# Feed-forward layer of a float32 transformer block: two plain token tiles, then seven tile pairs by Strassen's seven products

## The chip, the cores and the metric

The kernel runs on one core of one Trainium2 chip. The metric is device time in microseconds (us) of one execution: 2028.8 us before the change, the median of 3 runs (2028.22 to 2028.88). Views of the profile come from one profiled execution of the same kernel. The engines are PE (TensorE, matmul; PEld is its weight load), ACT (ScalarE), DVE (VectorE), POOL (GpSimd) and SP (SyncE, whose queue issues nearly all DMAs here).

## The reference

The input x has 8 sequences of 1024 tokens with 512 channels, the context 8 x 64 keys with 384 channels; all is float32.

```python
x = x + attention(layernorm(x), ctx)        # 16 heads, output projection Wo, bias bo
xn = layernorm(x)
hidden = xn @ W1 + b1                       # 512 -> 2048
imag = w_imag * sin(phases + 0.1 * hidden)
gain = cos(phases) * w_real + sin(phases) * w_imag
act = relu(hidden + gain * imag * 0.1)
x = x + act @ W2 + b2                       # 2048 -> 512
```

## The kernel before, in words

Tokens are taken in 16 tiles (`TILES`) of 512 (`TOK`). First comes attention for all tiles, which leaves x plus attention in HBM (`x1_dram`); then the feed-forward layer, tile by tile. Every float32 product is made of three matmuls of fp32r operands (`product`, lines 1394 to 1396): each operand is split into a rounded part (`hi`, ScalarE) and the rest (`lo`, VectorE), and hi x hi, hi x lo and lo x hi are summed in PSUM.

The feed-forward layer has `FC` = 16 chunks of 128 hidden channels for each tile. All of W1 and W2, in hi and lo, stays in SBUF. The step j = 16 t + f does the following:

- TensorE: `h = W1[f] x xt` into bank f % 4: 4 blocks of input channels x 3 matmuls = 12 matmuls of 512 columns. Then `second(j - 3)`: act x W2[f] into banks 4 to 7, which hold the tile's 4 output blocks over all 16 chunks: 4 x 3 = 12 matmuls.
- ScalarE: `turns` (the phase in turns, from PSUM, line 1010), `hid` (from PSUM, line 1012), the sine (`sine`, line 995), the relu that is also the hi split (`finish`, line 1001).
- VectorE: the whole number of turns (line 1350), `hid += gain * sine` (`wave`, line 1320), the lo split (`finish`, line 1325).
- GpSimd: turns minus whole turns (line 820), between VectorE's line 1350 and ScalarE's sine.

Beside that, each tile has once: its rows from HBM, the biases (GpSimd, lines 637 and 645), statistics (VectorE, line 1049), normalising (ScalarE, line 865), a transposition that consists of 32 x 32 transposes (VectorE, lines 1379 and 1384) and a way through HBM in 128-byte pieces, the split into `xt_hi` and `xt_lo`, and four additions of the outputs (`residual`, line 1313).

The order on each engine is written out by hand in Python loops, one per engine; all sync is by counting semaphores. An engine's instructions run in the order of its list, and a wait holds everything behind it. Queue SP does the same with DMAs: each `dma_start` waits for its semaphores, and those behind it wait too. What limits how far TensorE runs ahead is PSUM (4 banks for `h`) and the ring of 4 `act` buffers (`ACTS`).

## Time and profile before

| what | value |
|---|---|
| median of the runs | 2028.8 us |
| the profiled execution's span | 2027.3 us |
| what lies around the span (median minus span) | 1.5 us |
| PE busy | 2014.9 us (99%) |
| DVE busy | 1342.4 us (66%) |
| ACT busy | 1131.6 us (56%) |
| POOL busy | 1021.5 us (50%) |
| DMA moved | 168.51 MB, mean 83 GB/s |

The profile's page begins with busy time by engine, gives it then in 40 equal slices, then the DMA queues, the chain of waits that ended last, and the costliest groups of instructions (line, engine, operation, output <- inputs, count, busy and mean time, idle time before them and who ended it). A matmul's duration is longer than the distance from one to the next, since they are pipelined; so the distance of starts is what to read. The feed-forward layer begins at 630.3 us. Attention before it is not changed but for a few DMAs.

### The profile page before, as it was taken

Reading aid. Unit: us, or ns where it says so; the run is one execution under the profiler, and the core shown is the slowest. Engines: PE = TensorE matmul, PEld = TensorE weight load, DVE = VectorE, ACT = ScalarE, POOL = GpSimd, SP = SyncE. Lnnn points to the kernel's source line nnn. Section 1 sums busy time; section 2 is a strip of 40 time slices with the busy share of each in tenths; the row PEclk is TensorE's granted clock in tenths of the full one; section 3 lists DMA queues with packets and bytes.
Section 4 is the critical chain, followed back from the end, with each engine's and each line's share of the span. In section 5 each row is a group of like instructions: output and inputs, shape, how many; then the busy total and the mean of one; then the engine's idle time right before and its main releaser. Section 6 shows DMA issues by size and latency. Waiting matters only on the chain.

```text
span 2027.3 us, 26664 instructions
## 1 busy us (share of the span) xinstructions
PE 2014.9 (99%) x9498; PEld 1684.9 (83%) x9498; DVE 1342.4 (66%) x1983; ACT 1131.6 (56%) x1979; POOL 1021.5 (50%) x708
## 2 busy tenths in 40 slices
PE   9999999999999999999999999999999999999999
PEld 7788888888888888888888888888888888888887
DVE  8988888888876665655555555565655555555554
ACT  6767767667665655544554454545545454554453
POOL 6877777777774453435334343433435334343521
PEclk9999999999999999999999999999999999999999
DMA  7565675655524311121111212211130211112100
GB/s 240 150 164 136 169 175 138 173 137 164 143 66 144 107 42 42 45 81 27 57 42 42 54 40 73 42 42 42 42 83 21 64 43 42 46 48 73 42 22 21
DMA packets 232822, 168.51 MB, mean 83 GB/s; under 512 B 154353, under 2 KB 184049, under 8 KB 232689
## 3 DMA queue, kind: packets, MB, share of 16 engines
q1 hardware_dynamic: 231824, 166.76, 29.8%
q8 instruction: 75, 1.23, 0.3%
q14 instruction: 59, 0.48, 0.1%
q10 hardware_dynamic: 864, 0.04, 0.0%
HBM read 98.34 MB, written 68.16 MB: 82 GB/s over the span
## 4 chain that ended last, share of the span: by engine, by line
PE 91%; DVE 4%; ACT 2%; POOL 1%; issue 1%; DMA 1%; SPq 0%; ACTq 0%; DVEq 0%; POOLq 0%
PE psum L1394 29%; PE psum L1396 29%; PE psum L1395 29%; PE psum L1487 2%; DVE hid L1320 1%; POOL prob L679 0%; DVE act_lo L1325 0%; POOL prob L700 0%; ACT act_hi L1001 0%; ACT hid L1012 0%; DVE top L1177 0%; DVE prob L1168 0%; DMA x_sb<-in_x 0%; DVE xt_lo L1067 0%; DVE xt_lo L1277 0%
## 5 line engine op out<-in xcount | busy, mean ns | idle before, releaser
L820 POOL TENSOR_TENSOR frac<-turns,frac 128x512 f32<-128x512 f32 x256 | 333.3, 1302 | 826.9 <-DVE frac L1350 826.9
L1320 DVE SCALAR_TENSOR_TENSOR hid<-frac,gain,hid 128x512 f32<-128x512 f32 x256 | 321.7, 1257 | 144.2 <-ACT frac L995 143.1
L1394 PE MATMUL psum<-w_hi,act_hi 128*128 128x512 f32 x1024 | 398.3, 389 | 0.0
L1395 PE MATMUL psum<-w_lo,act_hi 128*128 128x512 f32 x1024 | 398.3, 389 | 0.0
L1396 PE MATMUL psum<-w_hi,act_lo 128*128 128x512 f32 x1024 | 398.3, 389 | 0.0
L1010 ACT ACTIVATE turns<-psum,u_shift 128x512 f32<-128x512 f32 x256 | 176.5, 689 | 328.4 <-PE psum L1396 271.2
L1001 ACT ACTIVATE act_hi<-hid 128x512 fp32r<-128x512 f32 x256 | 161.8, 632 | 353.9 <-DVE hid L1320 353.9
L1325 DVE SCALAR_TENSOR_TENSOR act_lo<-hid,act_hi 128x512 fp32r<-128x512 f32 x256 | 197.6, 772 | 178.1 <-ACT act_hi L1001 178.1
L1350 DVE TENSOR_SCALAR frac<-turns 128x512 f32<-128x512 f32 x256 | 111.4, 435 | 248.1 <-ACT turns L1010 248.1
L1395 PEld LDWEIGHTS psum<-w_lo,act_hi 128*128 128x128 f32 x1024 | 192.3, 188 | 40.0
L1394 PEld LDWEIGHTS psum<-w_hi,act_hi 128*128 128x128 f32 x1024 | 192.1, 188 | 39.9
L1396 PEld LDWEIGHTS psum<-w_hi,act_lo 128*128 128x128 f32 x1024 | 192.1, 188 | 39.8
L1394 PE MATMUL psum<-xt_hi,w1a_hi 128*128 128x512 f32 x512 | 199.5, 390 | 0.5 <-DVE xt_lo L1067 0.3
L1396 PE MATMUL psum<-xt_hi,w1a_lo 128*128 128x512 f32 x512 | 199.2, 389 | 0.0
L1395 PE MATMUL psum<-xt_lo,w1a_hi 128*128 128x512 f32 x512 | 199.2, 389 | 0.0
L1396 PE MATMUL psum<-xt_hi,w1b_lo 128*128 128x512 f32 x512 | 199.2, 389 | 0.0
L1394 PE MATMUL psum<-xt_hi,w1b_hi 128*128 128x512 f32 x512 | 199.2, 389 | 0.0
L1395 PE MATMUL psum<-xt_lo,w1b_hi 128*128 128x512 f32 x512 | 199.2, 389 | 0.0
L1012 ACT ACTIVATE hid<-psum,par 128x512 f32<-128x512 f32 x256 | 174.5, 682 | 0.0
L995 ACT ACTIVATE frac<-frac 128x512 f32<-128x512 f32 x256 | 161.4, 630 | 0.0
L700 POOL TENSOR_TENSOR prob<-prob,top 128x1024 f32<-128x1024 f32 x64 | 122.1, 1907 | 73.2 <-DVE top L1177 73.1
L679 POOL TENSOR_TENSOR prob<-prob,inv 128x1024 f32<-128x1024 f32 x64 | 123.6, 1931 | 42.1 <-DVE inv L1159 42.0
(149 smaller groups left out, 4013.1 us busy)
## 6 DMA issues: line engine op xcount, KB each, us to landing
res<-in_x SPq DMA_DIRECT2D x64, 256.0 KB, 3.8
x_dram<-res SPq DMA_DIRECT2D x64, 256.0 KB, 3.1
x_sb<-in_x SPq DMA_DIRECT2D x15, 1024.0 KB, 6.4
x_sb<-x_dram SPq DMA_DIRECT2D x15, 1024.0 KB, 5.5
xn<-turn_dram SPq DMA_DIRECT2D x30, 512.0 KB, 5.1
out<-x_sb SPq DMA_DIRECT2D x15, 1024.0 KB, 4.4
turn_dram<-kt SPq DMA_DIRECT2D x112, 128.0 KB, 2.4
x_sb<-turn_dram SPq DMA_DIRECT2D x28, 512.0 KB, 6.3
```

What stands on the lines that cost most here:

```text
L679: pool.tensor_tensor(rows, rows, inv[:, (i - 1) % 2, :].unsqueeze(2) .to_broadcast([P, NB * HG, KEYS]), ALU.mult).then_inc(prob_done, 1)
L700: pool.tensor_tensor(rows, rows, top[:, i % 2, :].unsqueeze(2).to_broadcast([P, NB * HG, KEYS]), ALU.subtract).then_inc(shift_done, 1)
L820: pool.tensor_tensor(frac[:, j % 2, :], turns[:, j % 2, :], frac[:, j % 2, :], ALU.subtract)\
L995: act.activation(frac[:, j % 2, :], frac[:, j % 2, :], ACT.Sin, scale=SIN_SCALE).then_inc(sin_done, 1)
L1001: act.activation(act_hi[:, j % ACTS, :], hid[:, j % 2, :], ACT.Relu).then_inc(act_hi_done, 1)
L1010: act.activation(turns[:, j % 2, :], hidden, ACT.Identity, bias=u_shift[:, f:f + 1], scale=0.1 / TWO_PI).then_inc(turns_done, 1)
L1012: act.activation(hid[:, j % 2, :], hidden, ACT.Identity, bias=par[:, 3, f:f + 1])\
L1320: dve.scalar_tensor_tensor(out=hid[:, j % 2, :], in0=frac[:, j % 2, :], scalar=gain[:, f:f + 1], in1=hid[:, j % 2, :], op0=ALU.mult, op1=A ...
L1325: dve.scalar_tensor_tensor(out=act_lo[:, j % ACTS, :], in0=hid[:, j % 2, :], scalar=0.0, in1=act_hi[:, j % ACTS, :].bitcast(F32), op0=ALU. ...
L1394: pe.matmul(o, a_hi, b_hi, start=first, stop=False)
L1395: pe.matmul(o, a_hi, b_lo, start=False, stop=False)
L1396: return pe.matmul(o, a_lo, b_hi, start=False, stop=last)
```

## The change

The two plain tiles (0 and 1) keep the 16 steps of 24 matmuls. For the others, tiles 2T and 2T+1 form a pair (T = 1 to 7). The first product of the layer, W1 x xt, is seen as a 2 x 2 block product: two chunks of hidden channels x two halves of the input channels, times two halves of input channels x two tiles. Strassen's scheme needs 7 block products (`P1` to `P7`) of 6 matmuls each, in place of 8. A pair has 8 groups p (`FP`), each for hidden chunks 2p and 2p+1, of both tiles. So one group gives four chains of elementwise work (kinds 0 to 3: chunk 2p and 2p+1 of the first tile, then 2p+1 and 2p of the second).

TensorE's order in a group is P1, P6, P4, P2, P5, P7, then `second` of two chunks of the first tile that the group before made, then P3. The second tile's hidden chunks stay in SBUF (`late_hid`), and after the eighth group a sweep of `second` for all its chunks follows (14 of 16; the last two come in the next pair's first group).

What goes with that:

- The sums of W1 blocks are formed once, by GpSimd during the two plain tiles (`add_parts`: 4 for each group), split into hi and lo, and written to HBM (`w1s`); the unsummed parts are copied there too. W2, in hi and lo, is written to HBM (`w2s`). In the pairs W1's operands come back through a ring of 8 slots of 256 KB, one load for each product, and W2's through a ring of 4 slots of 512 KB, one load for each `second`.
- The sums of token operands (T1 to T4) are formed by GpSimd once for each pair, from 128x1024 tiles.
- The products' sums are finished by VectorE: five operations from PSUM in each group (`sum_u`, `sum_v`, `hidden_21`, `hidden_22`, `hidden_12`), and ScalarE copies P1 out of PSUM (`keep_p1`).
- GpSimd no longer takes part in the chain of each chunk. Rounding to whole turns moves from VectorE to ScalarE (`whole`), the subtraction from GpSimd to VectorE (`fraction`).
- The outputs have a buffer of their own (`acc`), filled by a further load of x1's rows.
- Part of the code under `If_ne` (rows with a NaN in attention) is rewritten; it is not executed with these inputs.

```diff
+PRODUCTS = ("P1", "P6", "P4", "P2", "P5", "P7", "P3")
+OPERANDS = ("B11", "B21", "T1", "T2", "T4", "T3", "B22")
+BANK_OF = {"P1": 0, "P2": 0, "P6": 1, "P7": 1, "P5": 2, "P3": 2, "P4": 3}
+W1_SLOTS = 8
+W2_SLOTS = 4
...
+        def events(T):                                # order on TensorE and SP
+            order = []
+            for p in range(FP):
+                i = (T - 1) * FP + p
+                order += [("product", i, name) for name in PRODUCTS[:-1]]
+                if p:
+                    order += [("second", first_half(T, 2 * p - 2), None), ("second", first_half(T, 2 * p - 1), None)]
+                else:
+                    order += [("second", second_half(T - 1, c), None) for c in range(SWEPT, FC)]
+                order.append(("product", i, PRODUCTS[-1]))
+            order += [("second", first_half(T, FC - 2), None), ("second", first_half(T, FC - 1), None)]
+            return order + [("second", second_half(T, c), None) for c in range(SWEPT if T + 1 < FFN_PAIRS else FC)]
...
+            def load_w1(n):                           # SP
+                if n >= W1_SLOTS:
+                    sp.wait_ge(prod, n - W1_SLOTS + 1)
...
+            def load_w2(e):                           # SP
+                c = e % FC
+                sp.wait_ge(f_psum, e - W2_SLOTS + 1)
...
+            for T in range(1, FFN_PAIRS):             # ScalarE
+                more = T + 1 < FFN_PAIRS
+                for p in range(FP):
+                    i = (T - 1) * FP + p
+                    keep_p1(i)
+                    if p:
+                        turn(i - 1, 3)
+                        positive(first_half(T, 2 * p - 1))
+                        sine(chain_at(i - 1, 3))
+                    turn(i, 0)
+                    hidden(i)
+                    for at, s, half in ((3, 0, 0), (3, 0, 1), (5, 1, 0), (5, 1, 1)):
+                        if more and p == at:
+                            ffn_rows(2 * T + 2 + s, half)
+                    sine(chain_at(i, 0))
+                    turn(i, 1)
+                    turn(i, 2)
+                    positive(first_half(T, 2 * p))
+                    sine(chain_at(i, 1))
+                    sine(chain_at(i, 2))
...
+                for p in range(FP):                   # VectorE
+                    i = (T - 1) * FP + p
+                    if p:
+                        hidden_12(i - 1)
+                        wave(chain_at(i - 1, 2))
+                    sum_u(i)
+                    if p == 1:
+                        add_outputs(2 * T - 1)
+                    if p:
+                        positive_lo(first_half(T, 2 * p - 1))
+                        fraction(chain_at(i - 1, 3))
+                        wave(chain_at(i - 1, 3))
+                    if more and p in (3, 5):
+                        layer_shift(TILES + 2 * T + 2 + p // 5)
+                    fraction(chain_at(i, 0))
+                    sum_v(i)
+                    hidden_21(i)
+                    hidden_22(i)
+                    wave(chain_at(i, 0))
+                    if more and p in (1, 2):
+                        layer_stats(TILES + 2 * T + 2, half_blocks(p - 1))
+                    if more and p in (3, 4):
+                        turn_late_rows(2 * T + 2, p - 3)
+                        layer_stats(TILES + 2 * T + 3, half_blocks(p - 3))
+                    if more and p in (5, 6):
+                        turn_late_rows(2 * T + 3, p - 5)
+                    fraction(chain_at(i, 1))
+                    fraction(chain_at(i, 2))
+                    positive_lo(first_half(T, 2 * p))
+                    wave(chain_at(i, 1))
...
+            def strassen(i, name):                    # TensorE
+
+                p, n, j = i % FP, at_prod(i, name) - 1, OPERANDS.index(MOVING[name])
+                pe.wait_ge(w1_in[n % W1_SLOTS], 16 * (n // W1_SLOTS + 2))
...
+                elif name == "P5" and i:
+                    pe.wait_ge(c12_done, i)
+                elif name == "P2":
+                    pe.wait_ge(p1_done, i + 1)
+                elif name == "P7":
+                    pe.wait_ge(u_done, i + 1)
+                elif name == "P3":
+                    pe.wait_ge(c22_done, i + 1)
```

ScalarE's list in a plain step of the kernel before (PSUM tile `h` is `psum`; one step's four instructions, and the next step's first):

```order
L1010 ACTIVATE turns<-psum,u_shift 128x512 [waits act_lo_done,frac_done,h_psum]
L1012 ACTIVATE hid<-psum,par 128x512
L995 ACTIVATE frac<-frac 128x512 [waits frac_done]
L1001 ACTIVATE act_hi<-hid 128x512 [waits f_psum,wave_done]
L1010 ACTIVATE turns<-psum,u_shift 128x512 [waits act_lo_done,frac_done,h_psum]
```

ScalarE's list in a group of a pair of the changed kernel, from kind 0's turns on (line 1384 is `whole`, 1408 `turn`, 1416 `hidden`, 1421 the sine, 1436 the relu, 1391 `keep_p1` of the next group):

```order
L1408 ACTIVATE turns<-psum,u_shift 128x512 [waits prod,frac_done]
L1384 ACTIVATE frac<-turns,round_col 128x512 [waits wave_done,turns_done]
L1416 ACTIVATE hid<-psum,par 128x512 [waits act_lo_done]
L1421 ACTIVATE frac<-frac 128x512 [waits frac_done]
L1408 ACTIVATE turns<-hid,p_shift 128x512 [waits c21_done,frac_done]
L1384 ACTIVATE frac<-turns,round_col 128x512 [waits wave_done,turns_done]
L1408 ACTIVATE turns<-late_hid,p_shift 128x512 [waits c22_done,frac_done]
L1384 ACTIVATE frac<-turns,round_col 128x512 [waits wave_done,turns_done]
L1436 ACTIVATE act_hi<-hid 128x512 [waits wave_done,f_psum]
L1421 ACTIVATE frac<-frac 128x512 [waits frac_done] x2
L1391 ACTIVATE p_sb<-psum 128x512 [waits v_done,prod]
```

Three of the four turns in a group now come from SBUF tiles that VectorE has written (the waits c21_done, c22_done, c12_done), where all came from PSUM; a further instruction, `whole`, stands between turns and VectorE's part.

VectorE's list in a plain step of the kernel before:

```order
L1350 TENSOR_SCALAR frac<-turns 128x512 [waits wave_done,turns_done]
L1320 SCALAR_TENSOR_TENSOR hid<-frac,gain,hid 128x512 [waits hid_done,sin_done]
L1325 SCALAR_TENSOR_TENSOR act_lo<-hid,act_hi 128x512 [waits act_hi_done]
L1350 TENSOR_SCALAR frac<-turns 128x512 [waits wave_done,turns_done]
L1320 SCALAR_TENSOR_TENSOR hid<-frac,gain,hid 128x512 [waits hid_done,sin_done]
```

VectorE's list around a border of two groups in the changed kernel (1834 is `fraction`, 1848 `wave`, 1855 the lo split, 1797 `sum_u`, 1805 `sum_v`, 1814, 1822 and 1829 the three `hidden_` sums, 1529 the shift of a later tile's rows):

```order
L1834 SCALAR_TENSOR_TENSOR frac<-frac,turns 128x512 [waits whole_done] x2
L1855 SCALAR_TENSOR_TENSOR act_lo<-hid,act_hi 128x512 [waits act_hi_done]
L1848 SCALAR_TENSOR_TENSOR hid<-frac,gain,hid 128x512 [waits sin_done]
L1829 TENSOR_TENSOR late_hid<-psum,late_hid 128x512 [waits u_done,prod]
L1848 SCALAR_TENSOR_TENSOR late_hid<-frac,gain,late_hid 128x512 [waits sin_done]
L1797 SCALAR_TENSOR_TENSOR late_hid<-psum,par,p_sb 128x512 [waits act_lo_done,p1_done,prod]
L1855 SCALAR_TENSOR_TENSOR act_lo<-hid,act_hi 128x512 [waits act_hi_done]
L1834 SCALAR_TENSOR_TENSOR frac<-frac,turns 128x512 [waits whole_done]
L1848 SCALAR_TENSOR_TENSOR late_hid<-frac,gain,late_hid 128x512 [waits sin_done]
L1529 SCALAR_TENSOR_TENSOR shift_rows<-mv,rstd 128x4 [waits rstd_done]
L1834 SCALAR_TENSOR_TENSOR frac<-frac,turns 128x512 [waits whole_done]
L1805 SCALAR_TENSOR_TENSOR late_hid<-psum,par,p_sb 128x512 [waits act_lo_done,prod]
```

The five sums from PSUM stand between the operations of the chains, and each of them releases a product of TensorE or a turn of ScalarE.

The SP queue in a group and at its border in the changed kernel (719 is `load_w1`, 745 `load_w2`, 701 and 707 the way of a turned tile through HBM):

```order
L719 DMA w_ring<-w1s 128x512 [waits prod] x7
L707 DMA x_sb<-turn_dram 128x16x64 [waits a_moved0]
L707 DMA x_sb<-turn_dram 128x16x64 [waits a_moved1]
L745 DMA w_ring<-w2s 128x1024 [waits w2_stored0,f_psum]
L745 DMA w_ring<-w2s 128x1024 [waits w2_stored1,f_psum]
L701 DMA turn_dram<-temps 32x4x256 [waits a_back0,a_turned]
L701 DMA turn_dram<-temps 32x4x256 x3
L719 DMA w_ring<-w1s 128x512 [waits prod] x7
```

Before, SP had between two tiles only the turned rows (8 + 2 DMAs), one store and one load; now 7 loads of W1 and 2 of W2 stand in each group, in TensorE's order.

## Rows read from the trace of the kernel before

**Rows 1.** The page: busy time, the clock by slices, the chain by engine.
```profile
PE 2014.9 (99%) x9498; PEld 1684.9 (83%) x9498; DVE 1342.4 (66%) x1983; ACT 1131.6 (56%) x1979; POOL 1021.5 (50%) x708
...
PEclk9999999999999999999999999999999999999999
...
PE 91%; DVE 4%; ACT 2%; POOL 1%; issue 1%; DMA 1%; SPq 0%; ACTq 0%; DVEq 0%; POOLq 0%
```

**Rows 2.** Windows: busy (x count) PE, PEld, DVE, ACT, POOL; clock, DMA share, GB/s.
```profile
630.30:673.00 42.70, 42.67 (x188) 35.37 (x189) 31.45 (x54) 28.46 (x50) 12.65 (x9) 1.00 0.32 100
...
1300.00:1400.00 100.00, 100.00 (x443) 82.80 (x442) 56.68 (x76) 50.11 (x83) 43.04 (x31) 1.00 0.20 52
```

**Rows 3.** Timeline, PE: first and last matmul of the feed-forward layer.
```profile
630.33 0.47 PE L1394 MATMUL psum<-xt_hi,w1a_hi 128*128 128x512 f32 x1 [0.26 <-DVE xt_lo L1067]
...
2023.53 0.39 PE L1396 MATMUL psum<-w_hi,act_lo 128*128 128x512 f32 x1
```

**Rows 4.** Timeline: one step of a tile; start, duration, idle before and releaser.
```profile
1305.45 0.39 PE L1396 MATMUL psum<-xt_hi,w1b_lo 128*128 128x512 f32 x1
...
1305.87 0.69 ACT L1010 ACTIVATE turns<-psum,u_shift 128x512 f32<-128x512 f32 x1 [1.71 <-PE psum L1396]
...
1306.46 0.68 ACT L1012 ACTIVATE hid<-psum,par 128x512 f32<-128x512 f32 x1
...
1307.03 0.63 ACT L995 ACTIVATE frac<-frac 128x512 f32<-128x512 f32 x1
...
1307.10 1.29 POOL L820 TENSOR_TENSOR frac<-turns,frac 128x512 f32<-128x512 f32 x1 [0.74 <-DVE frac L1350]
...
1307.69 1.24 DVE L1320 SCALAR_TENSOR_TENSOR hid<-frac,gain,hid 128x512 f32<-128x512 f32 x1 [0.67 <-ACT frac L995]
...
1308.97 0.63 ACT L1001 ACTIVATE act_hi<-hid 128x512 fp32r<-128x512 f32 x1 [1.31 <-DVE hid L1320]
...
1309.64 0.69 DVE L1325 SCALAR_TENSOR_TENSOR act_lo<-hid,act_hi 128x512 fp32r<-128x512 f32 x1 [0.70 <-ACT act_hi L1001]
```

**Rows 5.** Timeline: the last `wave`, with GpSimd idle.
```profile
2017.45 0.75 DVE L1320 SCALAR_TENSOR_TENSOR hid<-frac,gain,hid 128x512 f32<-128x512 f32 x1
```

**Rows 6.** One line's instructions each: ns min/median/max, first and last start.
```profile
L1320 DVE SCALAR_TENSOR_TENSOR hid<-frac,gain,hid x256: 735/1246/1834, 637.9 to 2017.4; 128x512 f32<-128x512 f32 x128
...
L1313 DVE TENSOR_TENSOR x_sb<-psum,x_sb x64: 675/681/692, 725.8 to 2024.0; 128x512 f32<-128x512 f32 x64
...
L1184 DVE TENSOR_TENSOR pt_lo<-psum,pt_hi x128: 629/681/695, 46.3 to 614.0; 128x512 fp32r<-128x512 f32 x128
...
L637 POOL TENSOR_TENSOR x_sb<-x_sb,bo_row x64: 1287/1739/1755, 616.3 to 1881.6; 128x512 f32<-128x512 f32 x64
...
L1049 DVE BATCH_NORM_STATS2 stats<-x_sb x128: 634/677/695, 3.8 to 1887.5; 128x6 f32<-128x512 f32 x128
...
L1379 DVE STREAM_TRANSPOSE stage<-xn x14: 1236/1237/1239, 771.7 to 1903.2; 128x1024 f32<-128x1024 f32 x14
...
L865 ACT ACTIVATE xn<-x_sb,shift_rows,rstd x64: 799/802/814, 625.1 to 1903.2; 128x512 f32<-128x512 f32 x64
```

**Rows 7.** Windows during one store of 1 MB, one load of 1 MB, the 128-byte pieces.
```profile
1339.00:1341.00 2.00, 2.00 (x10) 1.69 (x9) 1.14 (x2) 0.68 (x2) 0.00 (x0) 1.00 0.98 368
...
1344.00:1347.00 3.00, 3.00 (x15) 2.49 (x14) 1.15 (x3) 2.10 (x4) 0.23 (x1) 1.00 0.86 322
...
1310.00:1313.00 3.00, 3.00 (x15) 2.49 (x14) 0.76 (x2) 1.69 (x3) 0.46 (x1) 1.00 0.94 202
```

**Rows 8.** DMA issues: size and median us from issue to landing.
```profile
x_sb<-x_dram SPq DMA_DIRECT2D x15, 1024.0 KB, 5.5
...
stage<-in_w SPq DMA_DIRECT2D x32, 256.0 KB, 2.8
k_dram<-kt SPq DMA_DIRECT2D x4, 512.0 KB, 3.6
```

**Rows 9.** The chain of waits at the start of the feed-forward layer (start, us, what).
```profile
642.00 3.76 DMA stage<-in_w
```

More of the change, by code:

```diff
@@ new lines, in second_half, with plain_hid, turned_at, whole_rows @@
+        def second_half(T, c):
+            return 2 * FC * T + FC + c
+        def plain_hid(j):
+            return p1_sb[:] if j % 3 == 2 else hid[:, j % 3, :]
+        def turned_at(T):
+            return TURNED_TILES + T - 1
+        def whole_rows(T, half):
+            return NB + 2 * (T - 1) + half + 1
+        def plain_events():
+            order = []
+            for j in range(PLAIN * FC):
+                t, f = divmod(j, FC)
+                order.append(("chunk", j))
+                if f >= LAG_B:
+                    order.append(("second", j - LAG_B))
+                if f == FC - 1 or (t > 0 and f < LAG_B - 1):
+                    order.append(("second", j - LAG_B + 1))
+            return order
@@ L836, in _ @@
+            with pool.If_ne(count, P):
+                for s in range(2):
+                    pool.wait_ge(out_stored[s], 16 * (FFN_PAIRS - s))
+                pool.wait_ge(last_stored, 16 * NB)
+                for t in range(TILES):
+                    spoil(t)
         @block.scalar
@@ L1015, in _ @@
+            for j in range(PLAIN * FC):
+                if j == FC - 1:
                     for half in range(2):
[L1016 removed]
+                        act.wait_ge(a_back[half], 16 * (turned_at(1) + 1))
+                    act.wait_ge(h_psum, FC)
                     for k in range(KC):
[L1018 to L1020 removed]
@@ L1380, in _ @@
-                if t + 1 < TILES and f == turn_at(t, 1):
-                    dve.wait_ge(xn_done, TILES + t + 2)
-                    if t:
-                        dve.wait_ge(moved[0], 16 * NB * (t + 1))
-                    dve.transpose(turned(t, 1), to_turn[:, 1]).then_inc(turn_done, 1)
-            wave(TILES * FC - 1)
-            finish(TILES * FC - 1)
-            residual(TILES - 1)
+                if pair_summed(j) is not None:
+                    for half in range(2):
+                        sum_to_lo(pair_summed(j), half)
@@ new lines, in _ @@
+                if j in FIRST_XT_AT:
+                    operand_lo(1, FIRST_XT_AT.index(j))
+            j = PLAIN * FC
+            operand_lo(1, 5)
+            wave(j - 1)
+            operand_lo(1, 6)
+            positive_lo(j - 1)
+            for T in range(1, FFN_PAIRS):
+                more = T + 1 < FFN_PAIRS
+                for p in range(FP):
+                    i = (T - 1) * FP + p
+                    if p:
[26 more added lines that the diff above has]
+                    wave(chain_at(i, 1))
+                hidden_12(i)
+                positive_lo(first_half(T, FC - 1))
+                wave(chain_at(i, 2))
+                fraction(chain_at(i, 3))
+                positive_lo(second_half(T, 0))
+                add_outputs(2 * T)
+                positive_lo(second_half(T, 1))
+                wave(chain_at(i, 3))
+                for c in range(SWEPT if more else FC):
+                    if c + 2 < FC:
+                        positive_lo(second_half(T, c + 2))
+                    if more and c in XT_AT:
+                        operand_lo(T + 1, XT_AT.index(c))
+                if not more:
+                    add_outputs(2 * T + 1)
```

971 lines of the change are left out of this document (697 added, 274 removed).

## The prediction

> **What bounds the kernel now.** I read the page first: TensorE is busy 99% of the span, its clock stands at its upper level (2.4 GHz) in every slice, and 91% of the chain of waits is PE [rows 1]. The windows say the same of the part that changes: 100.00 us of 100 are PE, while VectorE has 57, ScalarE 50, GpSimd 43, and the DMA engines a share of 0.20 [rows 2]. So a matmul removed from the feed-forward layer is time removed, until something else becomes late. The price of a matmul is the distance of starts: the layer's first begins at 630.33 and its last at 2023.53 [rows 3]; with one more distance that is 1393.4 us for 256 steps x 24 = 6144 matmuls, 0.2268 us each. (A step is 5.44 us.)
>
> **What is removed.** Two tiles cost 2 x 16 x 24 = 768 matmuls before. A pair costs 8 groups x 7 products x 6 = 336 for the first product of the layer and 32 x 12 = 384 for the second: 720. That is 48 less in each of 7 pairs, 336 in all, the number by which the built order of TensorE is shorter too. 336 x 0.2268 = 76.2 us. Against the profiled execution's own span: 2027.3 - 76.2 = 1951.1 us, the floor if nothing stalls. The median of the runs is 1.5 us above that span; I add this at the end.
>
> **What is added to VectorE and ScalarE, and whether it hides.** From the rows: an operation of VectorE from PSUM takes 0.68 us, also while GpSimd works (675/681/692 and 629/681/695) [rows 6]; one with two SBUF inputs 0.69 to 0.75 with GpSimd idle [rows 4, 5]. ScalarE takes 0.63 to 0.69 us, and 0.59 from start to start when nothing holds the next [rows 4]. A handover between them costs about 0.04 us, from TensorE 0.2 (last matmul from 1305.45, turns at 1305.87, a distance of 0.23 between) [rows 4]. The `fraction`, `whole` and PSUM sums are new forms. I bound each new VectorE one by 0.68 (PSUM form) and 1.25 (the median of `wave` beside GpSimd [rows 6]) and take 0.75, since GpSimd is now idle in most of a group; `whole` by 0.63 and 0.80 (the row with bias from SBUF, line 865 [rows 6]), and take 0.65.
>
> A group has 66 matmuls, 14.97 us. With P1 starting at 0, P2 starts at 4.08, P5 at 5.44, P7 at 6.80, the two `second` at 8.17 and 10.89, P3 at 13.61. Walking through the two lists with these durations (a group without extras): P1's copy is ready at 2.2 (P2 wants it at 4.08); `sum_u` at 3.6 (P7: 6.80); the lo part that the later `second` needs at 4.7 (10.89); `sum_v` at 9.1, `hidden_21` 9.7, `hidden_22` 10.4 (P3: 13.61); the last `wave` at 14.6; then `hidden_12` of this group 0.9 into the next (P5: 5.44). No product waits. VectorE has 5 x 0.68 + 8 x 0.75 + 2 x 0.69 = 10.8 us in 14.97, ScalarE 16 instructions of about 0.63 = 10.
>
> What counts is not the busy share but the chain that the two hand to each other. When they are late, nothing of TensorE's holds them and the group is 18 serial steps (hidden_12, turn, whole, relu, lo, fraction, sine, turn, whole, fraction, sum_v, 21, 22, wave, two fractions, lo, wave) of 0.70 with handover: 12.7 us. So a late group catches up by 2.3 us. Against that stand the extras of a pair that lie in its groups: on VectorE 4 output additions (2.7), 8 statistics (5.4) and 4 transpositions of 1.24 (5.0), 13.1 us; on ScalarE 8 rows of 0.80, 6.4 [rows 6]. All laid end to end: 8 x 12.7 + 19.5 = 121.1 us, against 8 x 14.97 = 119.8 on TensorE. That is 1.3 us over; part of the extras lies beside one another, and a pair begins its groups with the two engines free, since in the sweep before (16 x 2.72 = 43.5 us) each `second` wants only a relu and a lo part, beside 7 operands to split. Walking groups 3 to 6 with their extras, the two engines run 2.9, 2.9 and 3.2 us late at the borders, and the smallest spare is P1's copy: 0.7 us before P2 of group 6. So the stall is 0 in this walk and 1.3 us a pair in the end-to-end sum; the upper end, with GpSimd's adds (below), is 5. I take 1.0 a pair, 7 us. This is the thin place: behind P2 stand P5, P7 and both `second` on TensorE's in-order list.
>
> **Operations taken off.** GpSimd's subtraction (1.29 us) goes from each chain and with it the slowed `wave` [rows 4]. It was hidden behind TensorE; I count nothing for it, but the walk above lives on it.
>
> **GpSimd's tile-wide adds.** A pair has 4 row biases, 4 output biases and 4 operand sums of 1024 elements. The 512-element add takes 1.74 us [rows 6], so 3.5 each, 42 us a pair. The rows show what VectorE loses beside them: `wave` ran beside GpSimd for 0.70 us (1307.69 to 1308.39) and took 1.24, where 0.75 is its time alone [rows 4, 5], so 0.5 lost in 0.7 of overlap. The adds in the groups start with P7's end, when VectorE does `sum_v`, 21 and 22 from PSUM, which the rows show unslowed; of the rest I expect one operation an add, 0.5 us, inside the catching up of 2.3. The operand sums fall into the sweep, where VectorE has 2.72 us for each lo part of 0.69. Counted: nothing; other end: 12 adds x 3.5 x 0.7 lost, half of it in front of a waiting product, less what is caught up, about 4 us a pair.
>
> The Trainium skill (SBUF — State Buffer, Who interferes with whom) speaks against this: GpSimd and a VectorE operation with two SBUF inputs take a common port pair as an exclusive lock, and the loser waits for the other's whole instruction. By it the `wave` above would have ended at 1308.39 + 0.75 = 1309.14, and the trace has it at 1308.93, so the lock is nearly but not fully what is seen. By that rule each of four back-to-back operand sums of 3.5 us would let only one VectorE operation through, one in 4.2 us where the sweep wants one in 2.72.
>
> **DMA.** A group needs 7 x 0.262 + 2 x 0.524 = 2.88 MB, 193 GB/s; a sweep 8.4 MB in 43.5 us, the same. Rows, outputs and turned tiles add 10.5 MB a pair, of which 4.2 MB are in 128-byte pieces. The engines moved 368 GB/s in a store and 322 in a load at shares of 0.98 and 0.86, 202 at 0.94 in the pieces [rows 7]. So a pair needs 37.8/345 + 4.2/202 = 110 + 21 = 131 us of 163: it fits. Each W1 load is issued 13.6 us or more ahead of its product, each W2 load in the sweep 8.2 us; landing takes 2.8 us for 256 KB, 3.6 for 512 KB, 5.5 for 1 MB that may stand in front [rows 8]: 3.6 + 3 is still below 8.2. Counted: 0. The first plain tile is tighter: 22 chunks (5.8 MB), 15 stores of W2 (7.9), 6 raw pairs (3.1), 4 stores of sums (4.2), rows, acc and b2 (2.4): 23.4 MB, and two turned tiles 4.2: at 322 and 202 GB/s 73 + 21 = 94 us in a tile of 87. A lag of some 7 us builds up; the loads there are issued two steps (10.9 us) ahead, so it is just covered, and the second tile gives it back. A start like the 3.76 us wait for a stage [rows 9] may come more often. Between 0 and 17 us (at 260 GB/s 90 + 21 - 87 = 24, less 7 of cover); I take 2. In plain steps ScalarE has 5 instructions and at most 2 splits and 2 rows, 5 x 0.6 + 1.2 + 1.6 = 5.8 against 5.44, twice; the ring of 4 takes that. Attention gets six 512 KB stores: 0.
>
> **Sum.** 1951.1 + 7 + 2 = 1960.1 of span, + 1.5 = 1961.6: 1962 us, 3.3% less than before.
>
> **Rivals.**
> (A) VectorE and ScalarE stall the groups by 4 us or more a pair, through GpSimd's adds or new forms near 0.85: 7 x 5 = 35 in place of 7, 1990 us (1970 to 1995). For it: 1.3 us over in the end-to-end sum and the slowed `wave`. Against it: PSUM forms are not slowed, and the adds stand behind P7.
> (B) DMA is the bound in the plain tiles: 17 in place of 2, 1977 us (1968 to 1985). For it: 94 us of work in 87. Against it: two steps of cover, and a second tile that is lighter.
> (C) Slower than before: the handover chain, not TensorE, sets a group. If `fraction` and `wave` take 1.25 us as `wave` does beside GpSimd, for a reason other than GpSimd, a group is 12.7 + 8 x 0.5 = 16.7 and a pair's groups 8 x 16.7 + 19.5 = 153 in place of 119.8: 7 x 33 = 233 over the floor, 2185 us. It decides from 76.2 / 7 = 10.9 us a pair, which is 0.15 us on each of those eight (0.90 in place of 0.75). Against it: 0.75 with GpSimd idle [rows 5] and 0.69 [rows 4].
> (D) The change doesn't do what it says: 6-matmul products, each with a wait on its load, cost as much as 8 would. A wait that is met costs nothing in the rows (no idle time of PE before matmuls of `second`, which wait too), so: 2029 us.
>
> **Chances.** Forecast (1952 to 1969) 64%; A 19%; B 9%; C 5%; D and anything else near no change 3%. What a measurement tells from no change here is 0.2%, 4 us. Faster by more than that: 64 + 19 + 9 + 1 of the last two = 93%; within it 2%; slower 5%. The range takes forecast, B and the nearer half of A: 1951 to 1984; the low end is the floor of 1952.6 less the spread of a median.
>
> **What would show it.** PE busy near 1939 us and 336 matmuls fewer; a group of 14.97 us from P1 to P1 and a sweep of 43.5; PE idle in front of P2 (releaser: P1's copy by ScalarE), P7 or P3 would be A, in groups 4 to 6 first; idle in front of a product or a `second` with a DMA as releaser is B, in the first 90 us of the layer; `fraction` near 0.75 us. The forecast is wrong if a group without extras is longer than 15.1 us, if PE waits more than 3 us a pair, or if the plain tiles take more than 180 us in place of 174.

## The result and the profile after: 1.1% faster, where 3.3% was forecast

| | before | changed kernel |
|---|---|---|
| median of the runs | 2028.6 us | 2007.2 us (2003.7 to 2008.2, 4 runs) |
| span of the profiled execution | 2027.3 us | 2005.4 us |
| ratio to the kernel before | | 0.9891, 95% interval 0.9877 to 0.9905 |

The changed kernel is faster by 1.1%, with the interval clear of 1. The forecast of 1962 us and its whole range (1951 to 1984) lie below the result. The floor of the prediction was a span of 1951.1 us, and the span stands 54.3 us above it.

The page of the changed kernel, and its costliest DMA issues (count, size, median us from issue to landing):

```profile
PE 1957.9 (98%) x9162; PEld 1625.9 (81%) x9162; DVE 1605.7 (80%) x2272; ACT 1261.5 (63%) x2132; POOL 749.9 (37%) x453
...
PE 56%; DVE 22%; ACT 11%; issue 9%; POOL 1%; DVEq 0%; DMA 0%; ACTq 0%; POOLq 0%
...
w_ring<-w2s SPq DMA_DIRECT2D x240, 512.0 KB, 4.1
w_ring<-w1s SPq DMA_DIRECT2D x392, 256.0 KB, 3.6
```

9162 matmuls against 9498 [rows 1] are the 336 fewer. The chain of waits went from 91% PE to 56%, with 22% on VectorE. Next, what TensorE waited for, over the whole span (total, times, longest):

```profile
PE psum L1983 <- DVE act_lo L1855: 26.1, 14, 2.6
PE psum L1983 <- DVE late_hid L1822: 3.6, 7, 0.6
...
PE psum L1983 <- ACT p_sb L1391: 1.9, 1, 1.9
```

Each row names the waiting engine, its tile and line, then what ended the wait. No wait on a DMA stands in this view. The DMA engines did become busy; the four stretches of the plain tiles (columns as in [rows 2]) read:

```profile
632.20:675.00 42.80, 40.86 (x167) 33.15 (x167) 38.36 (x58) 34.45 (x61) 16.97 (x12) 0.93 0.87 309
675.00:720.00 45.00, 45.00 (x200) 37.26 (x200) 41.08 (x58) 37.49 (x66) 19.32 (x15) 1.00 0.97 306
720.00:765.00 45.00, 43.93 (x194) 36.11 (x193) 33.39 (x48) 30.56 (x53) 18.64 (x15) 1.00 1.00 342
765.00:807.00 42.00, 42.00 (x185) 34.47 (x184) 32.44 (x27) 25.65 (x43) 16.20 (x6) 1.00 0.80 254
```

A share near 1 and 306 to 342 GB/s, yet PE is idle for 1.9 us in the first stretch and 1.1 us in the third only, and both times a VectorE operation is what it waited for.

Where the 54.3 us lie, by the starts of matmuls in the timeline:

| part | expected | measured | over |
|---|---|---|---|
| first matmul of the layer | 630.33 | 632.20 | 1.9 |
| two plain tiles, to the first P1 at 807.69 (744 matmuls) | 168.7 | 175.5 | 6.8 |
| pair 1 to 7 (720 matmuls, the last 744) | 163.3 (last: 168.7) | 173.4, 170.5, 168.8, 170.7, 168.8, 168.8, 173.1 | 10.1, 7.2, 5.5, 7.4, 5.5, 5.5, 4.4 |

So 45.6 of the 54.3 us are in the pairs. A pair in the middle loses them in three places: 0.7 us before P3 of the seventh group, 2.0 us before the first `second` after the eighth group, and 1.9 us in the sweep, some 13 to 15 us later. The rest is a lower clock behind such a gap (last section; four times in the pairs of this execution, 1.6 us each), and small delays in the first three groups.

### The profile page after: what moved, and what is told of

Its sections match the earlier page's. It is cut to its first block, busy times and chain, and to the rows that moved or that the text cites. A ratio compares the mean times of both kernels' runs of the same rounds, so it can differ in the third digit from the quotient of the medians.

```text
span 2005.4 us, 27939 instructions
## 1 busy us (share of the span) xinstructions
PE 1957.9 (98%) x9162; PEld 1625.9 (81%) x9162; DVE 1605.7 (80%) x2272; ACT 1261.5 (63%) x2132; POOL 749.9 (37%) x453
## 4 chain that ended last, share of the span: by engine, by line
PE 56%; DVE 22%; ACT 11%; issue 9%; POOL 1%; DVEq 0%; DMA 0%; ACTq 0%; POOLq 0%
PE psum L1983 18%; PE psum L1985 17%; PE psum L1984 17%; DVE frac L1834 4%; ACT turns L1408 3%; DVE act_lo L1855 3%; DVE hid L1848 3%; PE psum L2076 2%; ACT frac L1384 2%; DVE acc L1867 2%; DVE stats L1517 2%; ACT x_sb L1208 2%; ACT act_hi L1436 1%; DVE late_hid L1848 1%; DVE late_hid L1805 1%
## 5 line engine op out<-in xcount | busy, mean ns | idle before, releaser
L1983 PE MATMUL psum<-w_ring,act_hi 128*128 128x512 f32 x1024 | 403.7, 394 | 27.2 <-DVE act_lo L1855 26.1
L1985 PE MATMUL psum<-w_ring,act_lo 128*128 128x512 f32 x1024 | 402.1, 393 | 0.0
L1984 PE MATMUL psum<-w_ring,act_hi 128*128 128x512 f32 x1024 | 402.0, 393 | 0.0
L1983 PE MATMUL psum<-xo,w_ring 128*128 128x512 f32 x784 | 307.6, 392 | 6.0 <-DVE late_hid L1822 3.6
L1985 PE MATMUL psum<-xo,w_ring 128*128 128x512 f32 x784 | 305.8, 390 | 0.0
L1984 PE MATMUL psum<-xo,w_ring 128*128 128x512 f32 x784 | 305.6, 390 | 0.0
L1834 DVE SCALAR_TENSOR_TENSOR frac<-frac,turns 128x512 f32<-128x512 f32 x256 | 223.5, 884 | 68.9 <-ACT frac L1384 68.0
L1983 PEld LDWEIGHTS psum<-w_ring,act_hi 128*128 128x128 f32 x1024 | 194.1, 190 | 73.9 <-issue 33.7
L1985 PEld LDWEIGHTS psum<-w_ring,act_lo 128*128 128x128 f32 x1024 | 194.1, 190 | 40.8
L1984 PEld LDWEIGHTS psum<-w_ring,act_hi 128*128 128x128 f32 x1024 | 194.4, 190 | 40.0
L1384 ACT ACTIVATE frac<-turns,round_col 128x512 f32<-128x512 f32 x256 | 185.3, 724 | 13.4 <-DVE hid L1848 6.2
L1983 PEld LDWEIGHTS psum<-xo,w_ring 128*128 128x128 f32 x784 | 147.2, 188 | 46.0 <-issue 15.4
L1985 PEld LDWEIGHTS psum<-xo,w_ring 128*128 128x128 f32 x784 | 147.2, 188 | 30.8
L1984 PEld LDWEIGHTS psum<-xo,w_ring 128*128 128x128 f32 x784 | 147.3, 188 | 29.4
L1855 DVE SCALAR_TENSOR_TENSOR act_lo<-late_hid,act_hi 128x512 fp32r<-128x512 f32 x112 | 127.0, 1155 | 42.7 <-ACT act_hi L1436 42.7
L1848 DVE SCALAR_TENSOR_TENSOR hid<-frac,gain,hid 128x512 f32<-128x512 f32 x134 | 116.3, 868 | 26.9 <-ACT frac L1421 26.9
```

What stands on the lines that cost most here:

```text
L1384: act.activation(frac[:, q % 2, :], turns[:, q % 2, :], ACT.Identity, bias=round_col[:]).then_inc(whole_done, 1)
L1834: dve.scalar_tensor_tensor(out=frac[:, q % 2, :], in0=frac[:, q % 2, :], scalar=ROUND, in1=turns[:, q % 2, :], op0=ALU.subtract, op1=ALU.s ...
L1848: dve.scalar_tensor_tensor(out=rows, in0=frac[:, q % 2, :], scalar=gain[:, f:f + 1], in1=rows, op0=ALU.mult, op1=ALU.add).then_inc(wave_do ...
L1855: dve.scalar_tensor_tensor(out=act_lo[:, e % ACTS, :], in0=rows, scalar=0.0, in1=act_hi[:, e % ACTS, :].bitcast(F32), op0=ALU.max, op1=ALU ...
L1983: pe.matmul(o, a_hi, b_hi, start=first, stop=False, skip_group_check=resumed)
L1984: pe.matmul(o, a_hi, b_lo, start=False, stop=False, skip_group_check=resumed)
```

## What holds VectorE

The group of all `fraction` operations points at the fault: minimum, median and maximum in ns, first and last start.

```profile
L1834 DVE SCALAR_TENSOR_TENSOR frac<-frac,turns x256: 648/687/2894, 638.4 to 1953.9; 128x512 f32<-128x512 f32 x128
```

The median is 687 ns, as hoped for, but single ones take up to 2894. The timeline says when. First comes one output-bias add of GpSimd in the seventh group of the second pair, and VectorE at that time:

```profile
1079.82 2.40 POOL L913 TENSOR_TENSOR acc<-acc,b_row 128x1024 f32<-128x1024 f32 x1 [20.44 <-PE psum L1985]
```
```profile
1078.41 0.69 DVE L1834 SCALAR_TENSOR_TENSOR frac<-frac,turns 128x512 f32<-128x512 f32 x1
1079.79 2.98 DVE L1848 SCALAR_TENSOR_TENSOR late_hid<-frac,gain,late_hid 128x512 f32<-128x512 f32 x1 [0.70 <-ACT frac L1421]
1082.70 0.68 DVE L1834 SCALAR_TENSOR_TENSOR frac<-frac,turns 128x512 f32<-128x512 f32 x1
1083.30 0.74 DVE L1805 SCALAR_TENSOR_TENSOR late_hid<-psum,par,p_sb 128x512 f32<-128x512 f32 x1
```

A `wave` of 0.75 us took 2.98: it ended at 1082.77, 0.55 us after GpSimd's add had ended at 1082.22. The two had started within 0.03 us of each other. Now the operand sums at the start of that pair's sweep, and VectorE beside them:

```profile
1112.53 2.78 POOL L1130 TENSOR_TENSOR temps<-x_sb 128x1024 f32<-128x1024 f32 x1 [14.55 <-DVE acc L1867]
1115.38 2.71 POOL L1130 TENSOR_TENSOR temps<-x_sb,temps 128x1024 f32<-128x1024 f32 x1
```
```profile
1109.69 2.76 DVE L1867 TENSOR_TENSOR acc<-psum,acc 128x512 f32<-128x512 f32 x4 [1.34 <-PE psum L1985]
1112.36 0.68 DVE L1855 SCALAR_TENSOR_TENSOR act_lo<-late_hid,act_hi 128x512 fp32r<-128x512 f32 x1
1112.96 2.89 DVE L1848 SCALAR_TENSOR_TENSOR late_hid<-frac,gain,late_hid 128x512 f32<-128x512 f32 x1
1115.78 3.46 DVE L1855 SCALAR_TENSOR_TENSOR act_lo<-late_hid,act_hi 128x512 fp32r<-128x512 f32 x2
```

One VectorE operation gets done per GpSimd add: the first ends at 1115.85, 0.54 us after the first add (1115.31). These are not chosen examples: 73 operations of lines 1834, 1848 and 1855 run beside a tile-wide add in the layer and end after it, and all 73 end 0.55 to 0.56 us after it (0.54 here is rounding). These are also the microseconds in which `second` wants a lo part for every 2.72 us.

**Theory:** while GpSimd runs a tensor-tensor operation in SBUF, a VectorE operation with two SBUF inputs waits for the whole of it, and the next GpSimd add then waits for VectorE (the adds take 2.78 and 2.71 us here, 2.40 above). **Rivals:** the delay goes by the amount of work (bytes) on GpSimd, wherever it stands; the handover chain is simply too long; DMA traffic slows VectorE.

## Experiments: the adds made small

These four leave all instructions, semaphores and orders in place and shrink operands alone, so that their output is incomplete. Ratios are to the kernel before.

**e1_small_adds**: all tile-wide adds of the pairs.

```diff
 def add_row_bias(T, half):
+    w = 8 if T >= 2 * PLAIN else C
-    pool.tensor_tensor(rows, rows, bo_row...)
+    pool.tensor_tensor(rows[:, :, 0:w], rows[:, :, 0:w], bo_row[:, 0:w]...)
 def add_last_bias(T, half):
+    w = 8 if T >= 1 else C
+    rows = acc[:, T % 2, blocks, 0:w]
 def operand_sums(T, names):
+    pool.tensor_tensor(PLACE[name][:, :, 0:4], PLACE[a][:, :, 0:4], PLACE[b][:, :, 0:4], ALU.subtract)
```

> All of GpSimd's adds of the seven pairs (row biases of tiles 4 to 15, output biases from tile 1 on, the operand sums) are cut from 1024 elements to 16; waits and order stay. Their output is left incomplete. Lock theory (VectorE's operations with two SBUF inputs wait for the whole of a GpSimd add): the pairs' excess over TensorE's own time, 45.6 us, nearly goes: 1966 us, 1962 to 1972; no VectorE operation of the pairs above 0.8 us. Density theory (the two elementwise engines' lists are too long for a group, with or without GpSimd): 1990 to 2003. DMA theory (the ring loads hold TensorE or the lists): 2004 to 2008.

Measured: 1958.0 us (1957.5 to 1958.7), ratio 0.9652 (0.9636 to 0.9669), span 1955.7. Of TensorE's waits on a lo part one is left, in the plain tiles:

```profile
PE psum L1985 <- DVE act_lo L1857: 1.9, 1, 1.9
```

From 806 us on, through all seven pairs, TensorE has no wait at all that the view counts. Groups are 14.96 us, the sweep 43.52, a pair 163.2: the floor. The groups of VectorE's operations, from 806 us on, of the changed kernel (busy, mean ns):

```profile
L1834 DVE SCALAR_TENSOR_TENSOR frac<-frac,turns 128x512 f32<-128x512 f32 x225 | 193.7, 873 | 60.9 <-ACT frac L1384 60.1
L1855 DVE SCALAR_TENSOR_TENSOR act_lo<-late_hid,act_hi 128x512 fp32r<-128x512 f32 x112 | 127.0, 1155 | 42.7 <-ACT act_hi L1436 42.7
...
L1814 DVE TENSOR_TENSOR hid<-late_hid,psum 128x512 f32<-128x512 f32 x56 | 38.5, 687 | 1.9
```

and of e1:

```profile
L1836 DVE SCALAR_TENSOR_TENSOR frac<-frac,turns 128x512 f32<-128x512 f32 x224 | 151.1, 686 | 70.2 <-ACT frac L1386 70.2
L1857 DVE SCALAR_TENSOR_TENSOR act_lo<-late_hid,act_hi 128x512 fp32r<-128x512 f32 x112 | 76.8, 691 | 99.5 <-ACT act_hi L1438 99.5
...
L1816 DVE TENSOR_TENSOR hid<-late_hid,psum 128x512 f32<-128x512 f32 x56 | 38.5, 687 | 1.9
```

The forms with two SBUF inputs fall to 686 and 691 ns; the one with a PSUM input is 687 in both. The DMAs and the chain of handovers are unchanged in e1, and no wait is left, so neither was the cause. Whether the amount of GpSimd's work counts or its exclusive access this run does not tell.

**e2, e3, e4** shrink one kind each: the output biases of tiles 2 to 15 (e2: `w = 8 if T >= 2 else C`), the operand sums alone (e3), and in the plain tiles the W1 sums of groups 1 to 7 and the biases (e4):

```diff
 def add_parts(engine, p):                 # e4
+    w = 8 if p else 2 * P
-    engine.tensor_tensor(to, a, b, op)
+    engine.tensor_tensor(to[:, 0:w], a[:, 0:w], b[:, 0:w], op)
 def add_row_bias(T, half):
+    w = C if T >= 2 * PLAIN else 8
 def add_last_bias(T, half):
+    w = C if T >= 1 else 8
```

> Only the output-bias adds of tiles 2 to 15 are cut to 16 elements (left incomplete). Lock theory: the stall before P3 of a pair's seventh group (0.7 us) and that at the first second() after the eighth group (2.1 us, and 1.6 of low clock in some) go, in all seven pairs: about 3.5 x 7 = 24 us less, 1983 us, 1978 to 1990. The last pair, which has only these adds, then has no stall. Density and DMA theories: no change, 2004 to 2008.

> Only the four operand sums of each pair are cut to 32 elements (left incomplete). Lock theory: the 2.1 us stall in each of six sweeps goes, and so does the block of six VectorE operations at 2.8 us before the first pair with its 1.9 us stall before P2: 6 x 1.9 + 3 = 14 us less, 1993 us, 1988 to 1997. Density and DMA theories: no change.

> GpSimd's adds of the two plain tiles are cut: W1 sums of groups 1 to 7 and row and output biases there (left incomplete); the pairs are as they were. Lock theory: of the plain tiles' 6.8 us over TensorE's time, the stalls at 668 and 736 us with the low clock behind the first go, 5 us: 2002 us, 1999 to 2005. DMA theory (a share of 0.87 to 1.02 there): no change, 2005 to 2008.

| | median us | ratio (interval) | less than the changed kernel |
|---|---|---|---|
| e1 all in the pairs | 1958.0 | 0.9652 (0.9636 to 0.9669) | 49 |
| e2 output biases | 1978.8 | 0.9749 (0.9733 to 0.9766) | 28 |
| e3 operand sums | 1989.4 | 0.9808 (0.9792 to 0.9825) | 18 |
| e4 plain tiles | 2002.0 | 0.9859 (0.9842 to 0.9877) | 5, runs from 1997 to 2007 |

e2 and e3 make 46 of e1's 49 together. In e2's trace the gap before the first `second` after the eighth group and the one in the seventh group are gone, the one in the sweep is there; in e3's it is the reverse. The wait of 1.9 us at the start of the first pair (on P1's copy in the changed kernel, on a lo part some 12 us ahead of P1 in e2) stands in e1 and e3 in neither form, so it belongs to the operand sums.

e4's gain is about its own spread, but its trace says more than its median. The two waits of the plain tiles (at 668 and 736 us in the changed kernel) are gone, one of 0.5 us is left, and the stretch from the layer's first matmul to the first P1 takes 173.4 us in place of 175.5; a wait of 1.9 us before the first pair stays, with the operand sums. What hides it is TensorE's clock: this execution has seven stretches at the lower level in the layer, the changed kernel's has five. The four runs follow their mean granted clock: 2007.0 and 2004.5 us at 0.994, 1999.5 at 0.997, 1996.8 at 0.998.

## Experiments: the adds moved

All of these compute the full output.

**f1_output_bias_beside_psum** starts the add some 2 us later in its group, where VectorE reads PSUM:

```diff
                     if p >= FP - 2:
-                        pool.wait_ge(prod, at_prod(i, "P7"))
+                        pool.wait_ge(frac_done, chain_at(i, 0) + 1)
                         add_last_bias(2 * T, p - FP + 2)
```

> Full output; GpSimd's output-bias adds of the last two groups of each pair no longer start when P7 is done but when VectorE has done the first fraction of the group, so that each 2.4 us add lies beside sum_v, hidden_21 and hidden_22, which read PSUM. Theory of the exclusive SBUF access: these adds cost nothing there, as leaving them out did, 1978.8 us; some overlap with the next fraction is left, so 1980 to 1988. Rival, it is GpSimd's amount of work and not its place that delays: 2007, as the changed kernel.

Measured: 1982.0 us (1979.4 to 1982.4), ratio 0.9764 (0.9748 to 0.9781): 25 of e2's 28 us, with all the work done. GpSimd in the seventh group of the second pair, and VectorE:

```profile
1075.67 2.41 POOL L913 TENSOR_TENSOR acc<-acc,b_row 128x1024 f32<-128x1024 f32 x1 [22.51 <-DVE frac L1834]
```
```profile
1075.51 0.74 DVE L1805 SCALAR_TENSOR_TENSOR late_hid<-psum,par,p_sb 128x512 f32<-128x512 f32 x1
1076.29 0.69 DVE L1814 TENSOR_TENSOR hid<-late_hid,psum 128x512 f32<-128x512 f32 x1
1077.08 0.69 DVE L1822 TENSOR_TENSOR late_hid<-psum,late_hid 128x512 f32<-128x512 f32 x1
1077.69 0.95 DVE L1848 SCALAR_TENSOR_TENSOR hid<-frac,gain,hid 128x512 f32<-128x512 f32 x1
```

Three operations with a PSUM and an SBUF input run at 0.69 to 0.74 through the add, and the `wave` behind them loses 0.2. Place decides, not amount: the rival of f1 is refuted. The 3 us that are missing lie in the last pair (167.6 us for its first 720 matmuls, 163.2 in e2), where a wait of 2.7 us stands after the eighth group.

**f2_sums_spread_in_sweep** spreads the operand sums:

```diff
                 if more:
-                    pool.wait_ge(y2_done, NB * (2 * T + 1))
-                    operand_sums(T + 1, OPERAND_SUMS)
+                    pool.wait_ge(rows_psum, (NB - 1) * 2 * T + 1)
+                    for n, name in enumerate(OPERAND_SUMS):
+                        if n:
+                            pool.wait_ge(f_psum, second_half(T, 2 * n) + 1)
+                        operand_sums(T + 1, [name])
                 for half in range(2):
+                    if more:
+                        pool.wait_ge(f_psum, second_half(T, 8 + 2 * half) + 1)
                     add_last_bias(2 * T + 1, half)
```

> Full output; the four operand sums and the odd tile's output-bias adds are no longer issued back to back at the start of the second products' sweep but one by one over its steps, four of the six after the adds from PSUM. Theory of the exclusive SBUF access: VectorE's four late operations of the transition meet at most one add; two thirds of what leaving the sums out gave (17.7 us), so 1993 to 1999. Rival, the sums themselves or their consumers cost: 2005 to 2010, or later sums make the next pair's first product wait by 3 us a pair, 2025.

Measured: 1991.7 us (1990.5 to 1993.8), ratio 0.9817 (0.9801 to 0.9833); 15 of e3's 18 us, a little better than expected. The sweep is back at 43.6 us in five of six pairs.

**f3_lo_of_last_group_earlier** asks whether the lo part before the sweep is merely ordered too late on VectorE. In the last group `positive` (ScalarE) and `positive_lo` (VectorE) of chunk 14 go before `turn(i, 2)` and `fraction(chain_at(i, 2))`; VectorE's part of the edit reads:

```diff
                     fraction(chain_at(i, 1))
+                    if p == FP - 1:
+                        positive_lo(first_half(T, 2 * p))
                     fraction(chain_at(i, 2))
-                    positive_lo(first_half(T, 2 * p))
+                    if p < FP - 1:
+                        positive_lo(first_half(T, 2 * p))
```

> Full output; in the last group of a pair the rounding and the low part of chunk 14, which the first second() after the group reads, are made before the fraction of kind 2 instead of after it. GpSimd's adds stay. Theory that the delay by GpSimd is one GpSimd add long and the low part is just late: 1.5 to 2 us less wait in six pairs, 1995 to 2000. Rival, VectorE is behind by the adds whatever the order, and the wait moves to the next reader: 2004 to 2009.

Measured: 2005.0 us (2003.2 to 2006.7), ratio 0.9881 (0.9864 to 0.9897). My expectation was wrong here and the rival right. TensorE's waits:

```profile
PE psum L1989 <- DVE act_lo L1858: 26.1, 22, 2.3
```

It is the same 26.1 us as in the changed kernel, in 22 waits instead of 14: the first wait after the eighth group fell from 1.85 to 0.5 us, and the time came back as 0.5 us at the next chunk and a longer one (2.2) in the sweep. This reordering moved VectorE's deficit and did not remove it.

**f4_all_three_and_row_bias** is f1, f2 and f3 with one row bias a group, in groups 0 to 3, at f1's trigger:

```diff
-                    if more and p < 2:
-                        for half in range(2):
-                            pool.wait_ge(prod, ...)
-                            add_row_bias(2 * T + 2 + p, half)
+                    elif more and p in (0, 1, 3):
+                        pool.wait_ge(frac_done, chain_at(i, 0) + 1)
+                        add_row_bias(2 * T + 2 + p // 3, p % 2)
```

> Full output; the three edits of this call together, and the row-bias adds one a group instead of two, each beside the PSUM reads. Theory of the exclusive SBUF access: the adds of the pairs cost nearly nothing, so towards the 1958.0 of the kernel without them, with the transition before the first pair untouched (2 us) and some overlap left: 1962 to 1972. Rival, gains do not add up since another late operation takes over: 1980 or more.

Measured: 1965.1 us (1962.4 to 1967.0), ratio 0.9688 (0.9672 to 0.9704). From the first group to the last, groups of 14.96 and sweeps of 43.52; around the pairs two waits are left, at the edges that were not moved, 1.85 us before the first pair and 1.91 after the last group.

**g1_ends_too** moves those as well:

```diff
-            operand_sums(1, OPERAND_SUMS)
+            for n, name in enumerate(OPERAND_SUMS):
+                if n:
+                    pool.wait_ge(turns_done, PLAIN * FC - 4 + min(n, 2))
+                operand_sums(1, [name])
             for half in range(2):
+                pool.wait_ge(turns_done, PLAIN * FC - 1 + half)
                 add_last_bias(1, half)
...
-                    if more:
-                        pool.wait_ge(f_psum, second_half(T, 8 + 2 * half) + 1)
+                    pool.wait_ge(f_psum, second_half(T, 8 + 2 * half) + 1)
```

> Full output; the kernel of f4_all_three_and_row_bias with two more stretches spread: the four operand sums and two output-bias adds ahead of the first pair, issued there back to back, are tied to five turn steps of the second plain tile 5.4 us apart, and the output bias of the last tile goes into the last sweep. Theory of the exclusive SBUF access: the two waits left there (1.85 and 1.91 us) and the 1.4 us of low clock behind them go, 1965.1 becomes 1960 to 1963. Rival, the later operand sums hold up the first products of the first pair: 1966 to 1970.

Measured: 1964.0 us (1961.7 to 1966.1), ratio 0.9678 (0.9665 to 0.9691), not told apart from f4, above what I expected. The wait after the last group is gone (1.9 us). The one before the first pair came back as 0.97 us on an operand's lo part and 2.33 us on P1's copy. In this execution TensorE also waited once for a DMA in the pairs, 0.4 us for a load of W2.

## Experiments: the same adds in shorter instructions

**g2_adds_in_quarters** moves nothing. It separates "for the whole instruction" from "by the amount of work":

```diff
 def add_last_bias(T, half):
+    n = 4 if T >= 1 else 1                    # row biases: T >= 2 * PLAIN
+    for k in range(n):
+        part = slice(k * C // n, (k + 1) * C // n)
+        inst = pool.tensor_tensor(rows[:, :, part], rows[:, :, part], b2_row[:, part]..., ALU.add)
+    inst.then_inc(acc_biased, 1)
 def operand_sums(T, names):
+    for k in range(4):
+        part = slice(k * NB // 4, (k + 1) * NB // 4)
+        inst = pool.tensor_tensor(PLACE[name][:, part], PLACE[a][:, part], PLACE[b][:, part], ALU.subtract)
+    inst.then_inc(t_done, 1)
```

> Full output; the changed kernel with every output-bias and operand-sum add of the pairs, and the row biases of tiles 4 on, cut into four instructions of 256 elements in a row instead of one of 1024, at the same places. Nothing is left out, GpSimd does the same work. Theory of an access held for one instruction at a time: a blocked VectorE operation waits for about 0.6 us instead of 2.2, so that VectorE does one operation per 1.3 us instead of per 2.9 us beside them; most of the 49 us that the adds cost goes, 1968 to 1985. Rival, the cost goes by the bytes that GpSimd moves: 2002 to 2010. Rival, each short instruction has a fixed price and VectorE is held off in total for longer: over 2010.

Measured: 1960.8 us (1960.5 to 1962.5), ratio 0.9665 (0.9650 to 0.9680), better than the expected range. With the same bytes moved, 46 of the 49 us are gone, so both rivals, the amount of work and a fixed price of each instruction, are refuted. The operand sums, at the same place as above, and VectorE beside them:

```profile
1094.99 4.56 POOL L1140 TENSOR_TENSOR temps<-x_sb 128x256 f32<-128x256 f32 x4 [10.20 <-DVE acc L1878]
1099.63 5.56 POOL L1140 TENSOR_TENSOR temps<-x_sb,temps 128x256 f32<-128x256 f32 x4
```
```profile
1095.42 1.23 DVE L1859 SCALAR_TENSOR_TENSOR late_hid<-frac,gain,late_hid 128x512 f32<-128x512 f32 x1
1096.58 2.37 DVE L1866 SCALAR_TENSOR_TENSOR act_lo<-late_hid,act_hi 128x512 fp32r<-128x512 f32 x2
```

Now a blocked operation takes 1.2 us, not 2.9, and the two engines still alternate one for one, with GpSimd's piece at 1.1 to 1.4 us. GpSimd pays: 864.9 us busy in place of 749.9. In the pairs VectorE's five forms with two SBUF inputs (`fraction`, both `wave`, both lo parts) take 600.4 us in the changed kernel, 536.2 here and 472.5 in e1. So half of the 128 us of blocking in these forms is still there, and the operand splits, which have two SBUF inputs too, are even longer than in the changed kernel (median 1755 ns where it has 1214). My reading, which no run tests by itself, is that the blocking now comes in pieces that the 2.3 us of catching up in a group absorb. Of the 49 us that reached TensorE almost none is left: pairs 2 to 6 take 163.2 to 163.4 us, in the first there is a wait of 0.74 us, and in the last two of 0.24 and 0.49.

**g3_both**: g1's places and g2's quarters, `n = 4` in both, no other edit.

> Full output; g1's placing and g2's quarters together. Theory: the placing has taken nearly everything, the quarters add at most 2 us (first groups' small waits): 1959 to 1963. Rival, more GpSimd instructions meet more VectorE operations: 1964 or more.

Measured: 1960.5 us (1959.1 to 1962.5), ratio 0.9660 (0.9647 to 0.9674). Its median is the lowest of the full kernels, though g2 alone can't be told from it, and it lies in the range expected: 3.4% below the kernel before and 2.3% below the changed one (0.9660 / 0.9891 = 0.9767).

## Why the prediction was wrong

- **Removed: right.** 336 matmuls fewer, and in e1, g2 and f4 a group of 14.96 us and a sweep of 43.5, nearly throughout.
- **GpSimd's tile-wide adds, "Counted: nothing": this step failed.** It cost 49 us (e1), 7 a pair, beyond even the "other end" of 4. Three things were wrong in it. I took 0.5 us lost in 0.7 of overlap as a proportion, and "one operation an add, 0.5 us"; the traces show a wait for the whole add, 2.2 us. I said that the adds behind P7 lie beside the PSUM reads; the trace has the add at 1079.82 beside a `wave`, and the PSUM reads come only behind it, at 1083.30 (f1 put the add beside them). And I took the sweep as having room for the operand sums. In the trace VectorE is behind at its start: the four output additions (from 1109.69) and the last `wave` of the last group (1112.96) still stand among the lo parts that `second` wants, and the sums fall on that `wave` and the lo part behind it. In the other direction I had the price of an add too high: 2.40 us alone, 2.7 to 2.8 when the engines alternate, not 3.5.
- **The rule that I weighed and set aside was right.** The `wave` of [rows 4] ended at 1308.93, 0.54 us after GpSimd's operation (1308.39). I had compared with a full 0.75 us behind it and read the difference as "not fully" a wait. In the changed kernel blocked operations end 0.55 us behind the add too, and in the kernel before 235 of the 256 `wave` operations end 0.55 us behind GpSimd's operation (the other 21 take 0.75 us). So a blocked operation has less left to do than its whole duration, and the row of before had shown the complete wait. The Trainium skill (SBUF — State Buffer, Who interferes with whom) tells of this exclusive access. The trace agrees: its consequence of one VectorE operation per add is what the sweep shows, at 2.9 us rather than the 4.2 that I worked out.
- **The walk of the lists, no product waits: right without the adds, e1.** The 7 us for the extras (1.3 a pair in the end-to-end sum) were not there: 0. P1's copy, my smallest spare, made TensorE wait in the first pair alone, and not with small operand sums (e1, e3).
- **New forms at 0.75: right.** `fraction` takes 0.69 us, the sums from PSUM 0.69 to 0.75.
- **DMA in the plain tiles, 2 us: rival B refuted.** TensorE waited for no DMA there. The 6.8 us are two waits on VectorE (1.9 and 1.1), which the trace of e4 doesn't have, the lower clock behind the first and smaller delays, and 1.9 us come from a later start of the layer; e1's span, 4.6 us over the floor, has what is left of these.
- **Rival A was the mechanism**, named with the right suspect and too little weight (19%). It was also sized too small: 45.6 us in the pairs for its 35, and 2007 us lies above its 1970 to 1995. C is refuted by e1's groups of 14.96 us, D by the floor of 163.2 us a pair that e1 reaches.

What stays open: the size of the plain tiles' loss, whose experiment (e4) gained no more than its spread, and the start of the layer. Over the twelve profiled executions of the changed kernel and its variants the first matmul starts anywhere from 630.2 to 632.9 us, though none of the edits touches attention, with a wait of TensorE on ScalarE of 0.8 to 2.7 us just before it. So the 1.9 us differ from execution to execution, and what sets them is not known.

## What to carry to other kernels

When work is taken off GpSimd's chain but GpSimd keeps large SBUF operations, look at each of these as a wall for VectorE's operations with two SBUF inputs: one wall stopped one operation for up to the wall's whole length here (2.2 of 2.4 us). Either place it where VectorE reads PSUM, or cut it into short instructions; cutting needs no schedule and gave at least as much here (g2 1960.8 us, f4 1965.1), at the price of 15% more busy time of GpSimd. A median or mean hides this; the maximum of a group, and the end of the blocked operation against the end of GpSimd's, show it.
